# Mixing by 64x64 products in two quarters of the array in place of one block-diagonal 128x128 product

## The reference

```
w = weights[conditions]                          # 64 matrices of 64 x 64
y = einsum('bct,bcd->bdt', x, w)                 # the mixing
a = quant_dequant(y.reshape(-1, 512))            # e2m1 values, a power-of-two scale per 32 columns
wq = quant_dequant(weight)                       # 512 x 512
out = x + (einsum('mk,nk->mn', a, wq) + bias)
```

## Time and profile before

| what | value |
|---|---|
| median of the runs | 112.89 us |
| span of the profiled execution | 111.7 us |
| PE busy, matmuls | 95.7 us, 86% of the span |
| PE busy, loads of weights | 44.4 us, 40% |
| DVE busy | 95.3 us, 85% |
| ACT busy | 79.1 us, 71% |
| POOL busy | 25.3 us, 23% |
| L313, the mixing, on PE | 34.0 us in 64 passes |
| PE's share of the chain that ended last | 60%, of which L313 17% |

### The profile page before, as it was taken

How to read it: one execution, slowest core, us unless ns; L and a number is a source line. 1 busy time by engine, 2 the same in 40 slices (tenths; PEclk the granted TensorE clock), 3 DMA queues, 4 the chain that set the end, 5 groups by cost and what they waited for, 6 DMA issues and landing times.

```text
span 111.7 us, 2056 instructions
## 1 busy us (share of the span) xinstructions
PE 95.7 (86%) x471; PEld 44.4 (40%) x478; DVE 95.3 (85%) x152; ACT 79.1 (71%) x117; POOL 25.3 (23%) x51
## 2 busy tenths in 40 slices
PE   5992961959389999999999999999999799998980
PEld 4981321434045333623453363345334236433420
DVE  5889919999899549997999799799979999999551
ACT  3730389699953998699689949994999925853500
POOL 0254807042070341122800090003001103000000
PEclk9998599999958999999999999999999999999999
DMA  1992158473819394844699539995760846943594
GB/s 43 348 334 68 30 136 283 140 274 99 318 35 373 40 351 150 212 100 159 216 307 271 191 122 354 260 345 147 135 246 36 201 87 232 244 129 146 195 373 183
DMA packets 13872, 22.11 MB, mean 198 GB/s; under 512 B 3877, under 2 KB 4392, under 8 KB 13865
## 3 DMA queue, kind: packets, MB, share of 16 engines
q1 hardware_dynamic: 11682, 17.83, 45.4%
q0 software_dynamic: 1888, 3.67, 16.2%
q10 hardware_dynamic: 294, 0.53, 1.3%
HBM read 10.49 MB, written 8.39 MB: 169 GB/s over the span
## 4 chain that ended last, share of the span: by engine, by line
PE 60%; ACT 14%; SPq 10%; issue 7%; DMA 5%; ACTq 1%; DVE 1%
PE o_ps L289 20%; PE y_ps L313 17%; PE o_ps L293 7%; SPq L171 7%; DMA x_sb<-in_x_dram 5%; PE o_ps L291 5%; PE o_ps L282 4%; ACT z L373 4%; PE y_ps L289 3%; ACT aT L419 2%; ACT y_sb L409 2%; SPq L187 2%; ACT zone L430 2%; ACT y_sb L386 2%; ACT wT L461 1%
## 5 line engine op out<-in xcount | busy, mean ns | idle before, releaser
L313 PE MATMUL y_ps<-x_sb,mix 128*128 128x512 f32 (+1 forms) x64 | 34.0, 666 | 9.2 <-DMA x_sb<-in_x_dram 4.7
L289 PE MATMUL o_ps<-wT,aT 128*128 128x512 bf16 x106 | 27.6, 381 | 1.6 <-ACT aT L419 0.9
L187 POOL DMA_DIRECT2D mix<-in_L_cond_weights_dram x32 | 17.1, 537 | 31.1 <-issue 17.4
L373 ACT ACTIVATE z<-y_ps 128x512 bf16<-128x512 bf16 x32 | 17.8, 629 | 7.9 <-PE y_ps L313 7.8
L313 PEld LDWEIGHTS y_ps<-x_sb,mix 128*128 128x128 f32 x64 | 12.2, 208 | 22.8 <-issue 13.7
L419 ACT COPY aT<-o_ps 128x1024 bf16<-128x1024 bf16 (+1 forms) x16 | 13.6, 911 | 10.0 <-PE o_ps L282 9.9
L562 DVE TENSOR_TENSOR n_int<-y_sb,inv 128x1024 int16<-128x1024 f32 x16 | 19.5, 1218 | 0.1
L430 ACT ACTIVATE zone<-inv 128x2048 int16<-128x2048 int16 (+1 forms) x10 | 17.6, 1768 | 0.2 <-DVE inv L553 0.2
L289 PEld LDWEIGHTS o_ps<-wT,aT 128*128 128x128 bf16 x112 | 9.1, 97 | 15.3 <-issue 7.6
L582 DVE TENSOR_TENSOR a<-n_clip,zone 128x2048 bf16<-128x2048 int16 x8 | 9.8, 1223 | 5.1 <-ACT zone L430 5.1
L549 DVE TENSOR_TENSOR clamped<-low,s 128x2048 bf16<-128x2048 bf16 (+1 forms) x10 | 11.2, 1118 | 0.3
(11 more groups left out here) (44 smaller groups left out, 96.2 us busy)
## 6 DMA issues: line engine op xcount, KB each, us to landing
x_sb<-in_x_dram SPq DMA_DIRECT2D x8, 1024.0 KB, 5.5
out_dram<-x_sb SPq DMA_DIRECT2D x32, 256.0 KB, 2.1
x_sb<-o_sb POOLq DMA_DIRECT2D x6, 512.0 KB, 5.8
w_sb<-in_L_ffn_weight_dram ACTq DMA_DIRECT2D x2, 256.0 KB, 3.3
w_sb<-in_L_ffn_weight_dram SPq DMA_DIRECT2D x2, 256.0 KB, 3.7
mix<-in_L_cond_weights_dram POOLq DMA_DIRECT2D x32, 16.0 KB, 3.8
mix<-in_L_cond_weights_dram SPq DMA_DIRECT2D x32, 16.0 KB, 4.6
bias_f<-in_L_ffn_bias_dram SPq DMA_DIRECT2D x1, 2.0 KB
```

The source lines that it names most:

```text
L187: queue.dma_start(mix[half, slot, tiles.start + i // 2, half], table[bass.ds(row, 1), :, :].rearrange("o c d -> (o c) d")).then_inc(mix_in ...
L289: nc.tensor.matmul(banks[:, t, :], aT[:, t, c, :], wT[:, c, :], start=(c == 0), stop=False)
L313: nc.tensor.matmul(y_ps[:, t, :], mix[:, slot, t, :], tile_of(x_sb, (step - 1) * GROUP + t), start=True, stop=True).then_inc(y_ready, 1)
L373: nc.scalar.activation(blocked(z[:, slot, t, :]), permuted_high(src), ACT.Abs, scale=ZONE_GAIN).then_inc(z_ready, 1)
```

## The change

A tile's two batches become two products of 64x64 with 512 columns each, which read 64 partitions and write 64 partitions. Batch 0 uses the rows and columns 0 to 63 of the array, batch 1 the rows and columns 64 to 127: opposite quarters. `mix` shrinks to 64 columns a tile, without zeros, and the clearing by DVE with its semaphore and waits falls away. The tiles are taken in pairs, in the order (t+1, batch 0), (t, batch 1), (t, batch 0), (t+1, batch 1); the wait for `y_copied` of both tiles stands ahead of the pair, and `y_ready` is raised by the third and the fourth product. The loop on PE is unrolled.

```diff
-        mix = sb("mix", [P, 2, GROUP, P], F32)
+        mix = sb("mix", [P, 2, GROUP, C], F32)
...
-            if clear:
-
-                queue.wait_ge(mix_clear, 1)
...
-                queue.dma_start(mix[half, slot, tiles.start + i // 2, half],
+                queue.dma_start(mix[half, slot, tiles.start + i // 2, :],
...
+            def mix_batch(step, slot, t, h):
+                half = slice(h * C, (h + 1) * C)
+                return nc.tensor.matmul(y_ps[half, t, :], mix[half, slot, t, :],
+                                        tile_of(x_sb, (step - 1) * GROUP + t)[half, :], start=True, stop=True)
+
             def mix_tiles(step, slot, loads_of_slot, tiles=range(GROUP), first=False):
                 pe.wait_ge(x_in[slot], 16 * loads_of_slot)
-                for t in tiles:
+                for t in tiles[::2]:
...
-                        pe.wait_ge(y_copied, GROUP * (step - 2) + t + 1)
-                    nc.tensor.matmul(y_ps[:, t, :], mix[:, slot, t, :], tile_of(x_sb, (step - 1) * GROUP + t),
-                                     start=True, stop=True).then_inc(y_ready, 1)
+                        pe.wait_ge(y_copied, GROUP * (step - 2) + t + 2)
+
+                    mix_batch(step, slot, t + 1, 0)
+                    mix_batch(step, slot, t, 1)
+                    mix_batch(step, slot, t, 0).then_inc(y_ready, 1)
+                    mix_batch(step, slot, t + 1, 1).then_inc(y_ready, 1)
...
-            with pe.Fori(1, GROUPS // 2 - 1) as pair:
+            for pair in range(1, GROUPS // 2 - 1):
...
-            nc.vector.memset(mix[:, :, :, :], 0.0).then_inc(mix_clear, 1)
```

More of the change, by code:

```diff
@@ L114, in adaln_ffn_program @@
         stored = sem("stored")
-        ident_clear, ident_ready, mix_clear = sem("ident_clear"), sem("ident_ready"), sem("mix_clear")
+        ident_clear, ident_ready = sem("ident_clear"), sem("ident_ready")
         ones_ready, idle_ready = sem("ones_ready"), sem("idle_ready")
@@ L174, in rows_of, with load_mixes @@
             return rows
-        def load_mixes(queue, rows, mix_in, g, slot, tiles, clear=False, reused=True):
-            if clear:
-                queue.wait_ge(mix_clear, 1)
+        def load_mixes(queue, rows, mix_in, g, slot, tiles, reused=True):
             if reused:
@@ L202, in load_group @@
                     rows = rows_of(mybir.EngineType.SP, g, SP_TILES)
-                load_mixes(sp, rows, sp_mix_in, g, slot, SP_TILES, clear=first, reused=reused)
+                load_mixes(sp, rows, sp_mix_in, g, slot, SP_TILES, reused=reused)
             def store(step, t, done, count):
@@ L243, in _, with load_half @@
         def _(pool):
-            def load_half(g, slot, clear=False, reused=True):
+            def load_half(g, slot, reused=True):
                 rows = rows_of(mybir.EngineType.Pool, g, POOL_TILES)
-                load_mixes(pool, rows, pool_mix_in, g, slot, POOL_TILES, clear, reused)
+                load_mixes(pool, rows, pool_mix_in, g, slot, POOL_TILES, reused)
             def add_by_dma(step):
@@ L258, in add_by_dma @@
                 nc.gpsimd.memset(token[:, :], 0.0).then_inc(o_free, 1)
-            load_half(0, 0, clear=True, reused=False)
+            load_half(0, 0, reused=False)
             load_half(1, 1, reused=False)
```

## The result

The changed kernel takes 115.95 us, the median of 4 runs (114.58 to 116.39), where the kernel before takes 113.1 on the same chip (112.69 to 113.4). The ratio is 1.0214, with a 95% interval of 1.0134 to 1.0294. A second timing on another chip, with 6 runs against 17, gave 1.0179 (1.0106 to 1.0253). So it is slower, as forecast, but by about 2% and not by 4.7%. The profiled execution took 115.66 us with a span of 114.0, against a span of 111.7 before.

A forecast was written before the change was run, and what follows sets the result against it. PE was taken to bound the steady part; 0.57 + 2.52 + 1.92 + 0.32 for the mixing halves gave 5.33 us on a span of 111.7, so 117.0, or 118.2 us with 1.2 around it; range 112.3 to 123.

The forecast's parts named there:

- the order of starts: PE's mixing: passes start in program order, so a product cannot start ahead of the preceding product's second pass.
- five slots: Main case: a mixing half's eight passes take 5 starts of 0.43 us, where four were; 118.2 us, chance 0.36.
- a with b and c with d: A half's four products in program order, two passes each; forecast to lie as a, a+b, b+c, c+d, d.
- the rival with four slots: Mixing: all passes pair up, +0.05 a first half, +0.20 a second; 1.1 us more, 114.0 us, chance 0.24.
- the 1.2 us around the span: Whole kernel: time outside the profiled span, taken as unchanged, leading from a span of 117.0 to 118.2 us.
- The 0.10 us an edge: PE: a matmul using another share of the array than its neighbour loses 0.10 us at its edge.
- the 0.8 a step: Steady part: time taken from PE's step brings at most about 0.8 us, then DVE is the bound.
- The three new ones: Edges new in a step's mixing: out of the first half, into and out of the second; 0.10 us each.
- Six slots: Rival: second and third product of a half, writing one bank, are kept apart; 122.3 us, chance 0.10.
- Eight: Rival: passes in opposite quarters of the mixing do not overlap, eight slots a half; 131 us, chance 0.10.
- no difference: Rival: four slots in the mixing, edges and weight loads cost nothing; 112.4 to 113.4 us, chance 0.10.
- stream faster: Rival: a mixing pass over 64 rows takes 0.22 us, the bf16 pace; 109 us, chance 0.10.

The follow-up runs named there:

- the run with one quarter first: Changed kernel with two products of the upper quarter ahead of two of the lower, instead of by turns; 116.42 us, ratio 1.0257.
- the changed kernel with idle products: Changed kernel plus 40 idle products of 128 columns ahead of the mixing of group 2 and 16 ahead of group 4's; 115.13 us, ratio 1.0094.
- the order by tile: Changed kernel with both products of a tile standing together, so neighbours write one bank; 115.28 us, ratio 1.013.

## Why the prediction was right in its direction and too high in its size

**The failed step is the order of starts.** The prediction took five slots a half, "since an order of starts is what every row of PE shows". Those rows were of matmuls that all use the full array; none could show what two quarters do. The pairs of the profile after and the run with one quarter first show it: passes in opposite quarters start in pairs whatever stands between them in the program. In the changed kernel whole products still start in their order, a with b and c with d. The fifth slot came from the belief that a product cannot start ahead of the second pass of the one before it, and it can: b starts 6 ns after a, a whole slot ahead of a's second pass. Without the fifth slot, 0.43 us less in each half, the sum is that of the rival with four slots. So 4.2 of the 5.33 us forecast were the fifth slot, which did not come; the direction came out right by the edges, the small part of the sum. The Trainium skill (TensorE: Matmul & The Clock Gate, Part 3) gives starts some 4 ns apart for different tiles of the array; the pairs start 6 to 14 ns apart. Its rule that matmuls start in the order of the program does not hold in the run with one quarter first, and its rule for their ends fits the signals there.

**The terms of that rival.** It had +0.05 for a first half and +0.20 for a second; measured are +0.04, and +0.20 with the 0.10 in the transposes ahead of it. Its 1.1 us for the steady part came out as 1.22 in one profile and 1.30 in the other. Its time of 114.0 is short of the measured one by the start, by what the clock does, and by the 1.2 us around the span: that figure sets one execution's span against the median of others, and in all runs but that of the changed kernel with idle products 1.6 to 1.7 us lie around the span. With that the rival's time is 114.5, and that of five slots 118.6.

**Drains.** The 0.10 us an edge was right: 0.09 from the last pair to the transposes, 0.10 more for the transposes with the edge behind them, and 0.09 where a full-size bias matmul meets the 64x64 products. The run with the bias over 128 rows shows that the edges were there before the change too and cost 0.93 us a step, eight for the four bias matmuls, some 0.12 each. That is also more than the 0.8 a step that the prediction thought DVE would let through. The three new ones, 0.29, less the 0.05 by which the first distance of a first half fell, are the loss of 0.24 a step; streaming costs nothing, as four slots before are four slots after.

**The start.** The prediction had ACT's first read of group 2 two slots later, 0.86 us, and PE's entry only 0.1 later for it. The profile after in which the clock falls where it fell before has the first: the read comes 2.03 us behind the start of the mixing, where it came 1.23 behind before (this start is below), 0.80 more. The entry is 0.28 later, within the bounds of 0 and 0.9, but not for the reason given. It is set by ACT's copy of the second tile, which ends at 31.31, and no longer by x, which lands at 31.00. The first tile's copy, all that the first product of the kernel before needs, is done at 30.33. So the wait for both copies, which the prediction checked in a step and not at the entry, is what delays it; against the run with the loop written out it does so by 0.56. In the first profile, too, PE waits last for the second copy (32.29; POOL's matrices land at 31.68). The entry is 1.27 later there, and the step failed also in what it held constant, the clock. The start of the mixing in the kernel before:

```profile
19.26 3.70 PE L313 MATMUL y_ps<-x_sb,mix 128*128 128x512 f32 x8 [3.37 <-DMA x_sb<-in_x_dram]
```

**What was right to cost at nothing.** The code length (ratio 1.0008); the clearing, since POOL's first matrix is issued at 4.59 without it and at 4.82 with it, but also at 4.51 with it in the run with the loop written out, so that its removal moves nothing that shows; the wait for two copies in a step, where PE waits for nobody, though not at the entry.

**The other rivals.** Six slots fell with the four pairs, and the order by tile shows that one bank does not hold quarters apart, against what the prediction quotes for that rival. Eight fell with every step of 10.73, no difference with the drains. A pass of 64 rows does not stream faster: pairs are 0.43 us apart.

**What stays open.** The term-by-term difference is 1.40 us, 1.25%, and that of the order by tile against the run with the loop written out 1.7 us. The measured ratios, 1.0179 and 1.0214, are 2.0 and 2.4 us; their intervals begin at 1.0106 and 1.0134. About 0.3 to 1 us is thus not located. The place of the half clock goes with 0.9 us between two executions of the changed kernel; whether the change draws the dear places more often, or chance did, the runs don't settle.

## What to carry to other kernels

Look for changes of the array's shape in a stream of matmuls before looking at the work in them: here each edge cost about 0.1 us, a 3-row matmul padded to 128 rows gave back 0.93 us a step for nothing, and zeros in a block-diagonal product that already filled the passes cost no time that quarters could win. When rows show an order, ask whether they had a chance to show anything else: an order among matmuls on the whole array says nothing of two on different parts of it. A wait that is moved ahead of a pair can cost nothing in a steady step and 0.3 to 0.6 us at the entry, so it is to be checked at both. And where the start of a kernel has idle stretches on PE, compare two profiles only after looking where the granted clock fell in each.

## What the runs showed of the hardware that was not expected

- Passes in opposite quarters start in pairs, 6 to 14 ns apart, at 0.43 us a pair (four slots for eight passes, in three orders of the program, one of which lets the third product start ahead of the second).
- The signals of products come in the order of the program all the same: the third product's last pass starts at 20.03, its signal goes up at 21.49, the fourth's at 21.53.
- Two quarters write one bank at the same time, in opposite halves of its partitions, at no cost (step of 10.74 against 10.73).
- A bf16 matmul over 3 rows among matmuls over 128 costs two edges of 0.10 us; over 128 rows it starts 0.22 us behind its neighbour like any other.
- The lower clock falls on different stretches in executions of the same kernel. The changed kernel, twice: group 2 and the entry of the steady part in one profile, group 1 and the first steady step in the other, with spans of 114.0 and 113.1.
